# Laying the first half's mLSTM stage between the attention units of a one-core decoder layer

## Chip, cores and metric

One core of a Trainium2 chip runs the whole layer in one launch. The metric is device time in microseconds (us) from launch to the last result; lower is better. The engines are PE (TensorE, matmuls and transposes), DVE (VectorE), ACT (ScalarE), POOL (GpSimd) and SP (SyncE, which only issues DMAs). Each takes its own instructions strictly in order; they meet only at semaphores.

## What is computed

The reference is a decoder layer on x of 8 batches x 128 tokens x 128 features, with three residual blocks, each behind a layer norm without weights:

```python
x = x + attn(layernorm(x))            # 16 heads of 8, causal, "hyperbolic" distances:
#   d2 = |q|^2 - 2 q.k + |k|^2 ; ed = sqrt(d2) ; ns = |q|^2 + |k|^2
#   dist = where(ed<0.1, taylor, where(ed>2, 0.693+log(ed)+c*ns/4, ed*sqrt(1+c*ns)))
#   o = softmax(-beta*dist, causal) @ v ; then o @ Wo.T
x = x + mlstm(layernorm(x), ctx, ctx) # 4 heads of 32, q = norm(x), k = v = ctx
#   ig, fg = [q,k,v] @ kernel + bias ;  cs = cumsum(log_sigmoid(fg))        (per head, over tokens)
#   log_D[s,t] = cs[s] - cs[t] + ig[t] (t<=s) ;  m[s] = max_t log_D
#   C = (q.k/sqrt(32)) * exp(log_D - m) ;  n = max(|sum_t C|, exp(-m)) ;  h = C/(n+1e-6) @ v
#   then a layer norm of each head times a scale
x = x + moe(layernorm(x))             # 8 experts of 256, top 2, silu(g)*u, all experts computed
```

With a[t] = ig[t] - cs[t] the decay exponent becomes a[t] - runmax[s], where runmax is the running maximum of a, and m = cs + runmax. That form is used before and after.

## The kernel before

**Three stretches.** The attention is 16 units (`NU`); a unit is half the heads of one batch. Then come the mLSTM stage and the experts, both in two halves (`NCH` = 2 chunks `c` of 4 batches). A half of the mLSTM stage is `front(c, k)` (norm, transpose, gates, running sum and maximum), then per batch `rows(m)` and `outs(m)` (m = 0..3 for half 0, 4..7 for half 1), then `back(c, k)` (head norm, residual, next layer norm, transpose, router). The experts are passes z = 0..15: 8 experts over half 0, then 8 over half 1. `back(1, k)` is laid between passes z = 2 to 9.

**The attention is software-pipelined.** Each engine has a function `step(s)`, s = -1 (PE: -2) to 20, and in step s works on several units. In step s, in the order of each engine:

- DVE: copies PV's result of unit s-4 (`o_sb`, where it ends a batch), `da` of s (L927), `sel` of s (L932, a predicated copy), two reduces of the distance of s-2 into `nm` (L942, L944), `prod` of s (L949), `o_n` (L953), `x1` = x + attention (L965), `m_ge` of s+1 (L970), `dist` of s-1 (L981, a predicated copy).
- ACT: `e2` (L676) and `l1` (L681) of s+1, `pT` (exp, L686) of s-3, `oT` (L690), `sqn` of s+1 (L695), `lp` of s (L700), `wt` of s+1 (L704), `shift` of s-2 (L709), `ds` of s (L713).
- PE: scores n1 of s+1 (needs `sel` of s), scores d2 of s+2, the output product Wo, 24 PV matmuls of s-3, the transpose of `nm` of s-2 (into bank `PM`), the transposes of `dist` of s-2 with its shift (into `P3`), the transpose of `o_n`.
- POOL: adds the causal mask to `dist` of s-1 (L531, L532), then `m_gt` of s+1 (L540, one long compare).

Four steps stand in a hardware loop body: `steps` runs s = 5..12 as two iterations of four. After steps 13 to 19 `ACT_TAIL`, `DVE_TAIL` and `PE_TAIL` name the few parts of half 0 that follow: the norm after steps 13 and 14, the gates and the running sum after step 18 on DVE, `rows(0)` after step 19. `rows(1..3)`, `outs(0..3)`, `back(0, .)` and the whole of half 1 come after the steps, in an order written out by hand for each engine.

**The gates before.** PE forms them as 36 rows (heads in rows 0 to 3 and 32 to 35) by 512 tokens in one bank. DVE and ACT then work on 4 partitions x 512 elements: ACT abs, exp, ln (L734 to L737); DVE min, subtract, four scans for the running sum (L997 to L1002), `arow`, four scans for the running maximum (L1008 to L1011), a last add (L1013). PE transposes `arow` back to tokens, ACT copies it out (L740), and only then `rows` can start. ACT also spreads the transposed norm into a block-diagonal tile `xblk` (L727, four copies). In PE's `rows(m)`, per head a mask matmul and a matmul that subtracts the running maximum go into `exp_bank(m)`, then one wide product q.k goes into bank `P2`; ACT takes four exps (L749); DVE multiplies (L1020, `cT`); PE's `outs(m)` multiplies by ctx; DVE copies (L1026, `hs`).

**Other parts the change touches.** The values of v are copied from `vab` to `v_st` by DMA, two batches at a time, in SP's queue between the loads of the score stacks. POOL clears `arow`, `w1_mem` and `xblk[0]` behind its step 5 (L553 to L555), and clears `xblk[1]` and copies ctx (L565, L567) behind its last step. ACT's `l1`, `sqn` and `wt` take bias, or bias and scale, from columns of the constant tile `cf`:

```python
A(l1[:, p, :], e2[:, p, :], ACT.Ln, scale=LN_SHIFT, bias=col(K_SEPS))
A(row(sqn), ps2, ACT.Square, scale=col(K_R8), bias=col(K_R8))
A(wt[:, p, :], sqn[:, :], ACT.Square, bias=col(K_HALF))
```

Of the kernel before, what the change touches and what calls it, by code (L numbers as in the profile page):

```python
# [7 lines left out]
NT = B * S  # L8
# [23 lines left out]
ACT_TAIL = {13: [("front", 0, 0)], 15: [("front", 0, 2)], 16: [("front", 0, 3)], 19: [("front", 0, 4), ("rows", 0)]}  # L32
DVE_TAIL = {13: [("front", 0, 0)], 14: [("front", 0, 1)], 18: [("front", 0, 3)], 19: [("rows", 0)]}
PE_TAIL = {14: [("front", 0, 1)], 15: [("front", 0, 2)], 19: [("front", 0, 4), ("rows", 0)]}
# [12 lines left out]
C_COL = C_NSEL + XH  # L47
# [14 lines left out]
def constants():  # L62
# [8 lines left out]
    for h in range(XH):  # L71
        c[h, C_NSEL + h] = -1.0
# [25 lines left out]
    return c, b.astype(mybir.dt.np(mybir.dt.bfloat16))  # L98
# [16 lines left out]
def decoder_layer(nc, x, ctx, ctx_t, wq_t, wk_t, wv_t, wo_t, log_c, log_beta, ig_k, ig_b, fg_k, fg_b,  # L115
                  norm_scale, router_t, gate_w, gate_b, up_w, up_b, down_w, down_b,
                  const_f, const_b, stack_init, out):
# [5 lines left out]
    with es:  # L123
# [11 lines left out]
        def sem(name):  # L135
# [62 lines left out]
        v_st = [sb(f"v_st{k}", [128, PB, 144]) for k in range(2)]  # L198
# [10 lines left out]
        dist = sb("dist", [128, 4, UW])  # L209
# [11 lines left out]
        xblk = [over(split_mem, [128, CB, XH, S]), over(dist_mem, [128, CB, XH, S], at=4 * NT)]  # L221
        frow = over(split_mem, [36, 2, CT], at=3072)
        lf = over(proj_mem, [4, CT], at=4 * CT)
        cs = over(proj_mem, [4, CT], at=5 * CT)
        runmax_all = [over(w1_mem, [128, CT], at=c * CT) for c in range(NCH)]
        runmax = [t[0:4, :] for t in runmax_all]
        arow = over(proj_mem, [36, CT], at=7 * CT)
        aT = sb("aT", [128, NCH, CB, 36])
        enm = sb("enm", [128, NCH, CB, XH])
        dT = over(split_mem, [128, 2, XH, S], at=4096)  # L230
        cT = over(split_mem, [128, 2, XH, S], at=5120)
        hs = over(dist_mem, [128, CB, XH, XD + 1], at=6 * NT)
        hden = sb("hden", [128, 3, CB * XH])
# [3 lines left out]
        hst = over(dist_mem, [128, 8, CB * XH], at=6 * NT + 640)  # L237
# [25 lines left out]
        names = ("cf_in par_in cb_in wqkv_in misc_in ctx_in exp_in stack0 v0_in v1_in out_done qsplit_done "  # L263
# [4 lines left out]
                 "x1_done gt_done causal_done nmT_full t_full pv_done oT_full wo_full g_full abs_done l1p_done "  # L268
                 "a_done rT_full aT_done enm_done ex_full dT_done cT_done hs_done hq_done hr_done lg_full "
# [54 lines left out]
        def steps(eng, step, first, last, lo, hi, after):  # L324


            for s in range(first, lo):
                step(At(None, s))
            with eng.Fori(0, (hi - lo + 1) // 4) as i:
                for j in range(4):  # L330
                    step(At(i, lo + j))
            for s in range(hi + 1, NU + 5):
                if s <= last:
                    step(At(None, s))
                after(s)
# [51 lines left out]

        def exp_bank(m):

            return (P1 if m < CB else P3)[:, m % 2, :]  # L390

        def cross_bank(m):

            return (PO, PM)[m % 2][:, :] if m < CB else P1[:, m % 2, :]

        def back_banks(c):

            return (PM[:, :], PO[:, :]) if c == 0 else (P3[:, 0, :], P3[:, 1, :])
# [3 lines left out]
        def _(sp):  # L402
# [71 lines left out]
            sp.wait_ge(sm["v_done"], 2)  # L474
# [7 lines left out]
            for k in range(2):  # L482
                next_values(NP - 1, k)
# [11 lines left out]
        def _(pool):  # L495
            link = linker(pool, "chain_p")
            pool.memset(eps_col[:, :], LN_EPS)
            pool.memset(wg_raw[:, :, :], 0.0).then_inc(sm["init_done"], 1)
# [44 lines left out]
            def zeros(s):  # L543
                if s == 5:
# [951 lines left out]
```

## Time and profile before

| | before |
|---|---|
| time, median of 3 runs | 296.92 us (296.44 to 297.27) |
| the profiled execution: its own time | 297.92 us |
| its span, first to last instruction | 296.1 us |
| busy PE / DVE / ACT / POOL | 225.9 / 220.1 / 170.9 / 108.9 us |
| mean granted TensorE clock | 0.764 of full speed |
| first attention scores (PE) | 33.38 us |
| first expert matmul (PE) | 202.47 us |

Busy time is an average over stretches with different limits, so the stretches are read apart: attention from 33 us, its last steps and the mLSTM stage from about 120 to 202 us, the experts after that. The granted clock is given as a share of 2.4 GHz: 0.50 is 1.2 GHz, 1.00 is 2.4 GHz, and values between are a stretch that had some of both. Bracketed text at the end of a timeline row is how long that engine had stood idle and whose result ended it.

### The profile page before, as it was taken

What the parts mean: (1) busy time and instruction counts of PE and PEld (TensorE: products, weight loads), DVE (VectorE), ACT (ScalarE), POOL (GpSimd) and SP (SyncE); (2) the same over time, 40 slices, a digit from 0 to 9 for tenths busy, and PEclk for the clock granted to TensorE, in tenths of its full rate; (3) what the DMA queues carried; (4) which work ended last, traced back from release to release, by engine and by line L of the source; (5) the groups of instructions that cost most, each with busy time, mean ns of one, the idle gap of its engine ahead of it and who ended that gap; (6) DMA issues with size and microseconds to landing.
All of it is one profiled execution on the core that took longest, in us unless ns stands there. A gap on an engine that the chain in (4) does not pass through costs nothing.

```text
span 296.1 us, 5262 instructions
## 1 busy us (share of the span) xinstructions
PE 225.9 (76%) x1624; PEld 180.5 (61%) x1624; DVE 220.1 (74%) x544; ACT 170.9 (58%) x291; POOL 108.9 (37%) x140
## 2 busy tenths in 40 slices
PE   0768323889897878779658950997994999999994
PEld 0423222777686767564536720685893889888984
DVE  6777699998989989993591658387669967656554
ACT  3498899999899999937412561355131137232330
POOL 5233235777756766552830000001042224334400
PEclk9995555575557785555856995699599699999999
DMA  5309779770413300086000000000000000010001
GB/s 156 79 1 194 164 183 231 182 212 24 95 18 81 71 24 20 0 251 196 2 1 0 0 0 0 3 0 1 2 0 0 0 2 1 2 35 0 0 0 35
DMA packets 38084, 16.80 MB, mean 57 GB/s; under 512 B 19240, under 2 KB 36016, under 8 KB 38064
## 3 DMA queue, kind: packets, MB, share of 16 engines
q1 hardware_dynamic: 38064, 16.56, 22.4%
q8 instruction: 10, 0.16, 0.2%
q14 instruction: 10, 0.08, 0.1%
HBM read 10.39 MB, written 4.98 MB: 52 GB/s over the span
## 4 chain that ended last, share of the span: by engine, by line
PE 41%; DVE 19%; issue 13%; ACT 13%; POOL 8%; DMA 4%; SPq 1%; DVEq 0%; ACTq 0%; POOLq 0%
PE P L1180 29%; PE PM L1180 6%; PE PO L1180 6%; POOL m_gt L540 5%; ACT sqn L695 2%; POOL dist L532 2%; DVE dist_mem L932 2%; DMA stn<-n_split 1%; ACT dist_mem L676 1%; POOL dist L531 1%; DMA k_split<-split_mem 1%; DVE proj_mem L1002 1%; ACT dist_mem L704 1%; DMA x_sb<-x 1%; DVE dist L981 1%
## 5 line engine op out<-in xcount | busy, mean ns | idle before, releaser
L782 ACT ACTIVATE dist_mem<-P,gub 128x512 f32<-128x512 f32 x32 | 21.8, 687 | 54.5 <-PE P L1180 54.5
L579 POOL CAST whi<-wgu 128x512 fp32r (+1 forms) x16 | 10.3, 642 | 101.5 <-PE P L1180 101.5
L1109 DVE SCALAR_TENSOR_TENSOR dist_mem<-P,gub,dist_mem 128x512 f32<-128x512 f32 x32 | 23.6, 749 | 23.0 <-ACT dist_mem L782 23.0
L540 POOL TENSOR_SCALAR m_gt<-dist_mem 128x768 uint8<-128x768 f32 x16 | 34.3, 2145 | 8.2 <-issue 5.9
L1180 PE MATMUL P<-cf,dist 128*128 128x128 f32 x96 | 29.5, 392 | 8.9 <-ACT shift L709 8.9
L1180 PE MATMUL P<-xhi,whi 128*128 128x512 f32 x64 | 28.5, 446 | 4.6 <-DVE dist_mem L1109 4.0
L531 POOL TENSOR_TENSOR dist<-dist,cf 128x128 f32<-128x128 f32 x32 | 14.6, 457 | 41.2 <-DVE dist L981 41.2
L1180 PEld LDWEIGHTS P<-cf,dist 128*128 128x128 f32 x96 | 19.1, 199 | 15.5 <-ACT shift L709 11.5
L1180 PE MATMUL PO<-v_st,pT 128*64 128x9 f32 (+1 forms) x384 | 25.6, 241 | 3.4 <-ACT pT L686 3.4
L1180 PEld LDWEIGHTS PO<-v_st,pT 128*64 128x64 f32 x384 | 23.9, 187 | 6.3 <-ACT pT L686 3.9
L1180 PE MATMUL P<-xhi,wlo 128*128 128x512 f32 x64 | 26.9, 421 | 0.0
L1180 PE MATMUL P<-xlo,whi 128*128 128x512 f32 x64 | 26.9, 420 | 0.0
L1180 PE MATMUL P<-shift,cb 128*128 128x128 bf16 x96 | 26.8, 289 | 0.0
L1180 PE MATMUL P<-stn,stq 128*128 128x128 bf16 (+1 forms) x128 | 12.8, 271 | 12.9 <-DVE dist_mem L932 12.9
L582 POOL TENSOR_TENSOR wlo<-wgu,whi 128x512 fp32r<-128x512 f32 x16 | 20.7, 1293 | 2.9 <-POOL whi L579 2.9
L1180 PEld LDWEIGHTS P<-stn,stq 128*128 128x128 bf16 x128 | 10.5, 133 | 15.0 <-issue 14.6
L1180 PEld LDWEIGHTS P<-xhi,whi 128*128 128x128 f32 x64 | 13.1, 205 | 7.7 <-issue 5.3
L932 DVE COPY_PREDICATED dist_mem<-m_ge,P 128x768 f32<-128x768 uint8 x16 | 16.3, 1017 | 1.2 <-ACT dist_mem L704 1.2
L927 DVE SCALAR_TENSOR_TENSOR dist_mem<-dist_mem,P 128x768 f32<-128x768 f32 x16 | 15.2, 950 | 2.2 <-ACT sqn L695 1.4
L1180 PEld LDWEIGHTS PO<-proj_mem,dist_mem 128*128 128x128 f32 x128 | 16.0, 196 | 0.7
L1180 PEld LDWEIGHTS PM<-proj_mem,dist_mem 128*128 128x128 f32 x128 | 15.9, 196 | 0.9 <-DVE dist_mem L1109 0.3
L686 ACT ACTIVATE pT<-P,nbeta 128x768 f32<-128x768 f32 x16 | 14.2, 887 | 3.9 <-PE P L1180 3.8
(219 smaller groups left out, 592.2 us busy)
## 6 DMA issues: line engine op xcount, KB each, us to landing
q_split<-split_mem SPq DMA_DIRECT2D x16, 128.0 KB, 2.7
k_split<-split_mem SPq DMA_DIRECT2D x4, 512.0 KB, 3.6
stq<-q_split SPq DMA_DIRECT2D x16, 128.0 KB
stk<-k_split SPq DMA_DIRECT2D x16, 128.0 KB
v_st<-vab SPq DMA_DIRECT2D x8, 144.0 KB, 2.3
wgu<-gate_w SPq DMA_DIRECT2D x1, 1024.0 KB, 5.8
wgu<-up_w SPq DMA_DIRECT2D x1, 1024.0 KB, 9.4
x_sb<-x SPq DMA_DIRECT2D x2, 256.0 KB, 3.1
```

The lines of the kernel that those rows point to most:

```text
L531: pool.tensor_tensor(wideq, wideq, cm, ALU.add)
L532: last = pool.tensor_tensor(near, near, cm, ALU.add)
L540: pool.tensor_scalar(m_gt[:, g.k % 2, :], e2[:, g.k % 2, :], 4.0 - ATT_EPS, None, ALU.is_gt).then_inc(sm["gt_done"], 1)
L579: pool.tensor_copy(hi, w).then_inc(sm["whi_done"], 1)
L582: pool.tensor_tensor(lo, w, hi, ALU.subtract).then_inc(sm["w_ready"], 1)
L686: A(row(pT, t.k % 2), P3[:, :, 0:384], ACT.Exp, scale=nbeta[:, :]).then_inc(sm["pT_done"], 1)
L695: A(row(sqn), ps2, ACT.Square, scale=col(K_R8), bias=col(K_R8)).then_inc(sm["sqn_done"], 1)
L782: A(sil[:, f, :], P[:, 0, :], ACT.Silu, bias=gub[:, 0, bass.ds(e * FC + f, 1)]).then_inc(sm["sil_done"], 1)
L927: V.scalar_tensor_tensor(row(da, p), row(l1, p), 2.0, n1, ALU.mult, ALU.add).then_inc(sm["da_done"], 1)
L932: V.copy_predicated(row(wt, p), row(m_ge, p), n1).then_inc(sm["sel_done"], 1)
L1109: V.scalar_tensor_tensor(hT[:, 2 * slot + f, :], (P1, P2)[f][:, 1, :], gub[:, 1, bass.ds(e * FC + f, 1)], sil[:, f, :], ALU.add, ALU.mult) ...
L1180: return nc.tensor.matmul(out_, lhsT, rhs, start=start, stop=stop, **more)
```

## The change

- The loops over attention steps are written out (`steps` is a plain Python loop), and each engine's step has numbered places 1 to 7; tables `ACT_AT`, `DVE_AT`, `PE_AT` name what is laid at `(step, place)`.
- Half 0's mLSTM stage goes there: the statistics of each batch (`stat(b)`) in steps 8 to 12, the norm in step 13, the gates in step 14, running maximum and the first exponents in step 15, `rows`/`outs` 0 to 3 in steps 15 to 19, the head norm's start in 19 and 20. Half 1's statistics are in step 20.
- The gates are formed as tokens (partitions) by 8 numbers per batch: eight matmuls of 8 columns in place of two pairs of 512 columns. The running sum is one product with a triangular matrix `tri` over 16 columns. One transpose to 16 rows, one scan of 16 x 128 for the running maximum, one transpose back.
- `rows` on PE is split into `ex(m)` and `qk(m)`; q.k has one bank for each half (`P2` bank 0, `PM`), `outs` another.
- POOL writes the block-diagonal tile from SBUF (`blocks(c)`), half 0 behind its step 14, and copies ctx behind its step 10. The clearing of `arow` and `w1_mem` is gone.
- PV reads `vab` itself; the DMAs to `v_st` are gone. `l1`, `sqn`, `wt` take constants as numbers.
- The head norm subtracts the mean before it divides by the normalizer, and folds the normalizer in later.

```diff
+ACT_AT = {(13, 1): [("front", 0, 0)], (13, 7): [("front", 0, 2)], (14, 4): [("front", 0, 3)],
+          (15, 5): [("rows", 0)], (16, 2): [("front", 0, 4), ("rows", 1)], (16, 7): [("rows", 2)], (17, 7): [("rows", 3)],
+          (20, 7): [("front", 1, 0)]}
+DVE_AT = {(8, 7): [("stat", 0)], (9, 7): [("stat", 1)], (11, 7): [("stat", 2)], (12, 6): [("stat", 3)],
+          (13, 3): [("front", 0, 1)], (14, 3): [("front", 0, 3)], (14, 6): [("front", 0, 4)], (15, 1): [("front", 0, 5)],
+          (15, 5): [("front", 0, 6)], (15, 7): [("stat", 4)], (16, 5): [("rows", 0)], (16, 7): [("stat", 5), ("rows", 1), ("outs", 0)],
+          (17, 7): [("rows", 2), ("outs", 1)], (18, 7): [("rows", 3), ("outs", 2)], (19, 7): [("outs", 3), ("back", 0, 0)],
+          (20, 7): [("stat", 6), ("stat", 7), ("back", 0, 1)]}
+PE_AT = {(13, 5): [("front", 0, 1)], (14, 1): [("front", 0, 2)], (14, 4): [("front", 0, 3)], (14, 5): [("front", 0, 4)],
+         (15, 3): [("front", 0, 5), ("ex", 0)], (15, 5): [("ex", 1), ("qk", 0)], (16, 5): [("ex", 2), ("outs", 0), ("qk", 1)],
+         (17, 5): [("ex", 3), ("outs", 1), ("qk", 2)], (18, 5): [("outs", 2), ("qk", 3)], (19, 5): [("outs", 3)]}
...
-            with sp.Fori(2, NP) as bp:
+            for bp in range(2, NP):
                 for k in range(2):
                     next_stack(bp, k)
-                    next_values(bp - 1, k)
...
-                    pool.memset(arow[:, :], 0.0)
-                    pool.memset(w1_mem[:, :], 0.0)
                     pool.memset(xblk[0][:, :, :, :], 0.0).then_inc(sm["xblk0"], 1)
+            def blocks(c):
+                pool.wait_ge(sm["xT_done"], NO[1, c] + 1)
+                for h in range(XH):
+                    r = slice(h * XD, (h + 1) * XD)
+                    link(pool.tensor_copy(xblk[c][r, :, h, :], tok(xT, c)[r, :].rearrange("p (b s) -> p b s", b=CB)))
+                pool.sem_inc(sm["blk_done"], 1)
...
-                    A(l1[:, p, :], e2[:, p, :], ACT.Ln, scale=LN_SHIFT, bias=col(K_SEPS)).then_inc(sm["l1_done"], 1)
+                    A(l1[:, p, :], e2[:, p, :], ACT.Ln, scale=LN_SHIFT, bias=LN_SHIFT * ATT_EPS).then_inc(sm["l1_done"], 1)
-                    A(row(sqn), ps2, ACT.Square, scale=col(K_R8), bias=col(K_R8)).then_inc(sm["sqn_done"], 1)
+                    A(row(sqn), ps2, ACT.Square, scale=8 ** -0.5, bias=8 ** -0.5).then_inc(sm["sqn_done"], 1)
...
+            # DVE, front(c, k)
                 if k == 3:
+                    dve.wait_ge(sm["g_full"], c + 1)
+                    V.tensor_tensor(gpre[:, c, :, :], G[:, 0:32]..., gb[:, :]..., ALU.add).then_inc(sm["pre_done"], 1)
+                    link(V.tensor_scalar(f[1], gpre[:, c, :, XH:], 0.0, None, ALU.min))
+                if k == 4:
+                    dve.wait_ge(sm["l1p_done"], c + 1)
+                    V.tensor_tensor(gf[:, c, 2, :], gf[:, c, 1, :], gf[:, c, 0, :], ALU.subtract).then_inc(sm["lf_done"], 1)
+                    dve.wait_ge(sm["cs_full"], c + 1)
+                    V.tensor_copy(gf[:, c, 1, :], G[:, 32:48])
+                    V.tensor_tensor(aT[:, c, :]..., gpre[:, c, :, 0:XH], G[:, 32:48]..., ALU.subtract).then_inc(sm["aT_done"], 1)
+                if k == 5:
+                    dve.wait_ge(sm["ar_full"], c + 1)
+                    V.tensor_tensor_scan(runmax[:, c, :], R, one, -3e38, ALU.max, ALU.mult).then_inc(sm["rm_done"], 1)
...
+            # PE, front(c, k)
                 if k == 2:
-                    mm(G[0:36, :], wg[:, 0, :], tok(xT, c), stop=False)
-                    mm(G[0:36, :], wg[:, 1, :], tok(ctxT, c), start=False).then_inc(sm["g_full"], 1)
+                    for b in range(CB):
+                        mm(G[:, cols], tok(xT, c, b), wg_raw[:, 0, :], stop=False)
+                        last = mm(G[:, cols], tok(ctxT, c, b), wg[:, :], start=False)
+                if k == 3:
+                    mm(G[:, 32:48], tri[:, :], gf[:, c, 2, :]).then_inc(sm["cs_full"], 1)
+            def ex(m):   # waits rm_done (b = 0), em_done (b = 1), dT_done of m-2 (b >= 2)
+            def qk(m):   # waits blk_done and sel_done >= NU (m = 0), x1_done (m = 4), cT_done >= m
+                mm(qk_bank(m), tok(ctxT, c, b), xblk[c][:, b].rearrange("p h s -> p (h s)"))
```

The hand-written order behind the steps, now for half 1 with `back(0, .)` between:

```diff
-            steps(pe, step, -2, NU + 4, 5, 12, after)
-            rows(1) rows(2) outs(0) rows(3) outs(1) front(1, 1) outs(2) front(1, 2) outs(3) front(1, 4)
-            rows(4) rows(5) rows(6) outs(4) outs(5) rows(7) back(0, 5) outs(6) back(0, 6) outs(7)
+            steps(step, -2, NU + 4)
+            front(1, 1) front(1, 2) front(1, 3) front(1, 4) front(1, 5)
+            ex(4) qk(4) ex(5) back(0, 5) outs(4) qk(5) ex(6) back(0, 6) outs(5) qk(6) ex(7) outs(6) qk(7) outs(7)
```

## Rows read from the trace of the kernel before

**Rows 1.** Stretches: length, busy of PE, PEld, DVE, ACT, POOL; clock, DMA share, GB/s.

```profile
77.00:113.30 36.30, 30.47 (x330) 25.69 (x328) 33.98 (x67) 35.19 (x53) 22.99 (x31) 0.69 0.21 50
...
141.80:162.00 20.20, 13.45 (x102) 10.16 (x102) 11.19 (x25) 6.33 (x15) 8.75 (x10) 0.66 0.00 1
162.00:185.50 23.50, 12.68 (x84) 9.32 (x82) 15.43 (x46) 10.25 (x26) 0.00 (x0) 0.83 0.00 0
```

**Rows 2.** ACT's instructions grouped by line and shape: busy us, mean ns.

```profile
L695 ACT ACTIVATE sqn<-P,cf 128x768 f32<-128x768 f32 x16 | 15.7, 984 | 0.5 <-PE P L1180 0.5
L681 ACT ACTIVATE dist_mem<-dist_mem,cf 128x768 f32<-128x768 f32 x16 | 15.0, 936 | 0.5
...
L700 ACT ACTIVATE lp<-dist_mem 128x768 f32<-128x768 f32 x16 | 13.4, 838 | 3.5 <-DVE dist_mem L949 3.5
```

**Rows 3.** Timeline of DVE, attention steps 8, 13, 15: start us, us, what.

```profile
83.55 0.95 DVE L927 SCALAR_TENSOR_TENSOR dist_mem<-dist_mem,P 128x768 f32<-128x768 f32 x1
...
113.34 0.95 DVE L927 SCALAR_TENSOR_TENSOR dist_mem<-dist_mem,P 128x768 f32<-128x768 f32 x1
...
129.20 0.94 DVE L927 SCALAR_TENSOR_TENSOR dist_mem<-dist_mem,P 128x768 f32<-128x768 f32 x1
...
140.73 1.02 DVE L981 COPY_PREDICATED dist<-m_gt,dist_mem 128x768 f32<-128x768 uint8 x1
```

**Rows 4.** Timeline of DVE beside POOL's work, steps 6 and 13.

```profile
73.41 2.53 DVE L970 TENSOR_SCALAR m_ge<-dist_mem 128x768 uint8<-128x768 f32 x1
...
116.04 0.94 DVE L949 SCALAR_TENSOR_TENSOR dist_mem<-dist_mem 128x768 f32<-128x768 f32 x1
```

**Rows 5.** Timeline of POOL at the same two places.

```profile
73.72 1.80 POOL L555 MEMSET split_mem<- 128x2048 f32 x1
...
115.08 2.13 POOL L540 TENSOR_SCALAR m_gt<-dist_mem 128x768 uint8<-128x768 f32 x1
```

**Rows 6.** Timeline of DVE: norms, gate work, head norm, outside the attention's own instructions.

```profile
127.04 2.02 DVE L873 TENSOR_SCALAR xn<-x_sb,mv,rs 128x128 f32<-128x128 f32 x4
...
147.16 0.74 DVE L997 TENSOR_SCALAR split_mem<-P,gb 4x512 f32<-4x512 f32 x1
...
153.72 0.68 DVE L1013 TENSOR_TENSOR proj_mem<-proj_mem,w_mem 4x512 f32<-4x512 f32 x1
...
164.96 0.86 DVE L860 BATCH_NORM_STATS2 bst<-x_sb 128x6 f32<-128x128 f32 x4
...
167.69 1.11 DVE L873 TENSOR_SCALAR xn<-x_sb,mv,rs 128x128 f32<-128x128 f32 x4
...
174.11 0.30 DVE L1026 COPY dist_mem<-PM 128x132 f32<-128x132 f32 x1 [1.96 <-PE PM L1180]
...
177.03 0.69 DVE L1046 TENSOR_TENSOR split_mem<-split_mem,dist_mem 128x512 f32<-128x512 f32 x1
```

**Rows 7.** Timeline of PE: gates, PV, half 1's first rows, last outs, first expert.

```profile
136.50 1.92 PE L1180 MATMUL P<-xT,wg 128*36 128x512 f32 x2
...
145.04 1.13 PE L1180 MATMUL PO<-v_st,pT 128*64 128x9 f32 x24 [1.80 <-ACT pT L686]
...
184.55 0.61 PE L1180 MATMUL P<-cf,proj_mem 36*128 36x36 f32 x4 [10.48 <-DVE proj_mem L1013]
185.55 0.29 PE L1180 MATMUL P<-cb 128*128 128x128 bf16 x1 [0.38 <-ACT aT L740]
...
196.43 0.22 PE L1180 MATMUL P<-cb 128*128 128x128 bf16 x1
...
197.76 1.02 PE L1180 MATMUL P<-dist_mem,split_mem 128*128 128x512 f32 x2
...
199.91 1.06 PE L1180 MATMUL PO<-rw,dist_mem 128*128 128x8 f32 x8
200.82 1.06 PE L1180 MATMUL P<-ctx,split_mem 128*128 128x33 f32 x8
202.47 0.47 PE L1180 MATMUL P<-xhi,whi 128*128 128x512 f32 x1 [0.59 <-DVE dist_mem L1026]
```

More of the change, by code:

```diff
@@ L70, in constants @@
     c[:, C_CM:C_CM + HALF] = np.where(np.arange(HALF)[None, :] > (p % HALF)[:, None], FAR, 0.0)
-    for h in range(XH):
+    for h in range(CB * XH):
         c[h, C_NSEL + h] = -1.0
@@ L322, in pass_waits, with steps @@
             eng.sem_inc(sm["passed"], 1)
-        def steps(eng, step, first, last, lo, hi, after):
-            for s in range(first, lo):
+        def steps(step, first, last):
+            for s in range(first, last + 1):
                 step(At(None, s))
[L329 to L335, printed above, removed]
         def linker(eng, name):
@@ L585, in _ @@
             prepare(1, 1, 1)
+            pool.wait_ge(sm["t_full"], NU)
+            link(pool.memset(xblk[1][:, :, :, :], 0.0))
+            blocks(1)
             with pool.Fori(1, E // 2) as i:
@@ L662, in _, with at @@
                 last.then_inc(sm["v_done"], 1)
+            def at(s, place):
+                stages = dict(front=front, rows=rows, back=back)
+                for stage, *which in ACT_AT.get((s, place), ()):
+                    stages[stage](*which)
             def step(s):
+                k_ = s.k
                 u, t = s + 1, s - 3
@@ L783, in silu @@
                       bias=gub[:, 0, bass.ds(e * FC + f, 1)]).then_inc(sm["sil_done"], 1)
-            def after(s):
-                stages = dict(front=front, rows=rows, back=back)
-                for stage, *which in ACT_TAIL.get(s, ()):
-                    stages[stage](*which)
-            steps(act, step, -1, NU + 4, 5, 12, after)
-            rows(1)
-            front(1, 0)
-            rows(2)
-            rows(3)
+            steps(step, -1, NU + 4)
+            back(0, 0)
             front(1, 2)
+            back(0, 1)
             front(1, 3)
-            front(1, 5)
-            back(0, 0)
-            back(0, 1)
+            back(0, 2)
             front(1, 4)
@@ L905, in _, with at @@
                 V.tensor_scalar(nsl[:, c, :], ksl[:, :], col(K_M36), None, ALU.mult).then_inc(sm["split_done"], 1)
+            def at(s, place):
+                stages = dict(front=front, rows=rows, outs=outs, back=back, stat=stat)
+                for stage, *which in DVE_AT.get((s, place), ()):
+                    stages[stage](*which)
             def step(s):
+                k_ = s.k
                 def row(t, w):
@@ L1125, in weigh @@
                 last.then_inc(sm["y_done"], 1)
-            def after(s):
-                stages = dict(front=front, rows=rows, outs=outs, back=back)
-                for stage, *which in DVE_TAIL.get(s, ()):
-                    stages[stage](*which)
-            steps(dve, step, -1, NU + 4, 5, 12, after)
-            rows(1)
-            front(1, 0)
-            front(1, 1)
-            outs(0)
-            rows(2)
-            outs(1)
-            outs(2)
-            rows(3)
-            outs(3)
-            back(0, 0)
+            steps(step, -1, NU + 4)
+            front(1, 1)
+            back(0, 2)
             front(1, 3)
-            back(0, 1)
+            back(0, 3)
+            front(1, 4)
             front(1, 5)
+            front(1, 6)
+            back(0, 5)
             rows(4)
-            back(0, 2)
+            outs(4)
             rows(5)
-            back(0, 3)
-            outs(4)
-            back(0, 5)
+            outs(5)
+            back(0, 6)
             rows(6)
-            outs(5)
+            outs(6)
             rows(7)
-            outs(6)
-            back(0, 6)
             outs(7)
@@ L1226, in pair_count, with at @@
                 return m if u.i is None else u.i * each + m
+            def at(s, place):
+                stages = dict(front=front, ex=ex, qk=qk, outs=outs, back=back)
+                for stage, *which in PE_AT.get((s, place), ()):
+                    stages[stage](*which)
             def step(s):
+                k_ = s.k
                 u = s + 1
@@ L1423, in down @@
                 last.then_inc(sm["y_full"], 1)
[L1425 to L1435 removed]
+            steps(step, -2, NU + 4)
             front(1, 1)
[L1437 removed]
             front(1, 2)
[L1439 removed]
+            front(1, 3)
             front(1, 4)
[L1441 to L1443 removed]
+            front(1, 5)
+            ex(4)
+            qk(4)
+            ex(5)
+            back(0, 5)
             outs(4)
+            qk(5)
+            ex(6)
+            back(0, 6)
             outs(5)
[L1446 to L1447 removed]
+            qk(6)
+            ex(7)
             outs(6)
[L1449 removed]
+            qk(7)
             outs(7)
```

330 lines of the change are left out of this document (162 added, 168 removed).

## The prediction

> **What bounds the kernel now.** I read the stretches first [rows 1]. In attention steps 7 to 12 (77 to 113.3 us) ACT is busy 35.19 of 36.30 us, DVE 33.98, PE 30.47 at a mean clock of 0.69: ACT leads, DVE is 2.3 us behind it, and nobody has room. From 141.8 us to 185.5 us it is the reverse: 43.7 us in which DVE works 26.6, PE 26.1 and ACT 16.6. This stretch is a chain of waits, and that is where the change works. The DMA share there is 0.00, so the expert weights have long landed; loading them earlier, or sparing the `v_st` loads, buys nothing by itself. What makes the chain long is read in the timelines. DVE spends 147.16 to 154.40 us on half 0's gate rows, tiles of 4 partitions by 512, before it takes up the attention's last units [rows 6]. Later PE stands idle 10.48 us until DVE's L1013 has finished the same work for half 1, and starts its rows at 185.55 [rows 7]. Half 0's `rows` and `outs` run only after the attention steps, ending with DVE's copy at 174.11 [rows 6]. PE begins the experts at 202.47 [rows 7]. Behind that point nothing in the change alters the work of a pass.
>
> I count as three intervals. T is the end of the last `dist` copy on DVE (before: 140.73 + 1.02 = 141.75 [rows 3]); S is PE's first exponent matmul for batch 4 (185.55); M is the first expert matmul (202.47) [rows 7]. So before T to S is 43.8 us and S to M is 16.9 us.
>
> **1. Up to step 13 (`da` at 113.34 before [rows 3]).** Constants given as numbers: `l1` takes 936 ns and `lp`, the same work without a column operand, 838 [rows 2], so one such operand costs 0.10 us. `wt` loses one as well, `sqn` loses two (984 against 838 is 0.15, two operands would be 0.20). That is 0.35 to 0.40 us per unit on ACT. In steps 0 to 5, where DVE's load is lighter since `nm` and `o` are not there at first, I take 1.5 us of the possible 2.3 (bounds 0 and 2.3). In steps 7 to 12 DVE becomes the bound after 2.3 us [rows 1], and it is given four `stat(b)`: four statistics took 0.86 us together [rows 6], single ones each with a wait and an aggregate I take at 0.5, so 2.0 us (bounds 0.9 and 2.4). Six steps cost DVE 36.0 against 36.3 before: -0.2 (bounds -1.4 and +1.5).
>
> The cleared tiles: `m_ge` took 2.53 us from 73.41 [rows 4] and ended 0.4 us behind POOL's memset of `xblk` (73.72 to 75.52 [rows 5]). That memset, 2048 elements in 1.80 us, stays; the two that go (512 and 1024 elements) are 1.35 us at that rate. I take -1.0 (bounds 0 and -1.35), because PE has nearly as much to do there. Unrolling by itself, the 8-column gate weights formed at the start and the fewer DMAs: 0. The time between `da` of step 8 and of step 13, 83.55 to 113.34, is 5.96 us a step [rows 3], all of it accounted for by busy ACT and DVE, so a loop branch costs nothing to be won. The page "Runtime: NRT & Kernel Launch" of the Trainium skill (Instruction fetch mechanics) says that a taken branch out of the fetched window stalls the fetch and that kernels prefer unrolling for it; by that rule there would be a gain here, and the trace does not show one to be had. `da(13)`: 113.34 - 1.5 - 1.0 - 0.2 = 110.6.
>
> **2. Steps 13 and 14.** Before they took 15.9 us (113.34 to 129.20 [rows 3]), with half 0's statistics and norm in them. The norm stays (its four `xn` 2.02 us [rows 6]), the statistics leave (-1.2). New: in step 14 DVE waits at place 3 for the gates. PE forms them in 8 matmuls of 8 columns, each two instructions. The router's 8 instructions of that form, begun at 199.91, gave way to the next at 200.82 [rows 7]: 0.11 each at full clock, so 16 are 1.8 us, and 3.6 at half clock. The wide form cost 2 x 1.92 at most [rows 7], so on PE it is a draw; but now PV of unit 11, the `nm` transpose and DVE's `prod`, `m_ge` and `dist` stand behind it. I take +3.0 us (bounds 1.2 and 3.6). Then DVE waits in place 6 for three small ACT functions and for the triangular product and holds up `dist`: +1.2 (bounds 0.4 and 2.0). Six small DVE operations of 8 to 32 columns: the 132-column copy takes 0.30 [rows 6], I take 0.2 each, +1.2 (bounds 0.6 and 1.8). 15.9 - 1.2 + 3.0 + 1.2 + 1.2 = 20.1, `da(15)` at 130.7.
>
> **3. `da(15)` to T.** Before 12.55 us [rows 3], with the wide gates inside, 136.50 to about 139.9, ahead of Wo and PV on PE [rows 7]: -3.4. New on PE ahead of the last `dist`: `ex(0)`, `ex(1)`, `qk(0)`. An `ex` is 196.43 to 197.76, so 1.33 us; a `qk` 1.02 [rows 7], 0.9 start to start: +3.6, and DVE's `cT(0)`, +0.7. T = 130.7 + 13.4 = 144.1 (bounds: none of it visible 140; PE at half clock 148). POOL's four block copies stand behind `m_gt`, ahead of the next causal mask. They are hidden unless they end late; bound 0 to 2.4.
>
> These copies and the ctx copy also run beside DVE. A long POOL compare, 115.08 to 117.21 [rows 5], left DVE's two-input `prod` at 0.94 us, begun inside it at 116.04 [rows 4], while the memset did hold up `m_ge`. The Trainium skill's "SBUF — State Buffer" (two separate sides) says the port that DVE and GpSimd share is locked for a whole instruction, also against a DVE operation with two SBUF inputs when GpSimd reads SBUF. By that rule the copies would add up to their own 3.4 us; by the row, only one-input operations suffer. My sum has 0 for it and the bound above.
>
> **4. T to S.** PE has still: `ex` 2, 3 (2.7), `outs` 0 to 3 (1.06 [rows 7], 0.9 start to start: 3.6), `qk` 1 to 3 (2.7), PV of three units (1.13 each [rows 7]: 3.4), two units' transposes, which I estimate as long as PV with its hand-over (2.6), and some 1.5 for hand-overs: 16.5 us at full clock, in place of the same work one after the other behind the steps. Then a DVE chain: head norm start as from 174.41 to 177.72 before [rows 6], less one multiply of 0.7 (2.6); the last `x1` and half 1's statistics to `xn`, as 164.96 to 168.80 [rows 6] (4.1); the square on ACT and two reductions between them (1.9). PE has idled, so half clock: transposes and copy 1.2, gates 3.6; then sign, exp, ln 1.5; triangular product, copies, transpose, scan 2.0. 16.5 + 8.6 + 8.3 = 33.4 against 43.8 (bounds 29 and 38, by 0.1 or 0.3 us per small operation and the clock). The 7.24 us block and its twin are gone from the chain; `back(0,2)` and `back(0,3)` fill DVE's waits. S = 177.5.
>
> **5. S to M and on.** The same matmuls, with q.k in one bank, `qk(m)` waiting for `cT(m-1)`: 0.9 + 0.7 plus hand-overs is under the 3.1 us of PE a batch, hidden. 16.9 stays (bounds 14.5 and 18.5): M = 194.4, 8.1 us earlier. The experts' 93.6 us stay.
>
> **Sum.** The profiled execution took 297.92 (span 296.1), 1.0 above the median of 296.92. The same 8.1 us off gives 289.8 and 288.8; I say 288.8.
>
> **Rivals.**
> - *PE stays at half clock through the laid stage* (slower than before). The attention ran at a mean of 0.69, the next stretch at 0.66 [rows 1]. The 16.5 us of part 4 would be 33, since ex, outs and qk stand in PE's queue ahead of `nm` and PV, the attention's own chain: +14 to 16, 303 us. It decides above 8.1 us, that is if half of this work runs at half clock. Against: as PE gets denser (162 to 185.5, where rows and outs follow each other) the clock was 0.83 [rows 1]. Chance 0.10.
> - *Order waits eat half*: DVE, strictly in order, waits at place 3, 6 and 7 for PE and ACT, each time with the attention's `dist` or `nm` behind it, 4 us more than counted: 292.8. For it: part 3 and 4 leave each hand-over 0.1 to 0.2 us. Chance 0.20.
> - *Nothing to be seen*: what half 0 gains is given back because PE waits in S for half 1's norm anyway and the early part is lengthened by 8 us of stall: 296.9. Chance 0.04.
> - *More*: PE at full clock for both gates (-3.6), constants pay in all steps (-2): 283. Chance 0.14.
> - *Forecast*, 285.5 to 291: chance 0.52.
>
> **How the numbers follow.** A measurement of this kernel tells about 0.3% (0.9 us) from nothing. Faster: forecast, more, order waits, 0.86 in all; same 0.04; slower 0.10. The range reaches from the lower case's 283 to the end of the order waits at 295: 282.8 to 295.0, which leaves 0.14 above and some 0.05 below.
>
> **What the profile after would show.** `sqn` near 0.79 us, `l1` and `wt` near 0.84; `m_ge` of step 6 under 1.6; `da(13)` near 110.6; an idle of DVE of 1 to 3.5 us in step 14 ended by PE; no DVE operation on 4 x 512; T near 144; S near 177.5, M near 194.4. Wrong if PE's clock in 135 to 160 us is near 0.5, if T comes after 150, or if the expert passes take longer than 93.6 us.

## The result, and the profile after

The changed kernel takes 330.52 us (median of 4 runs, 329.93 to 333.15) against 297.10 for the kernel before (4 runs, 296.44 to 297.49): ratio 1.1168, 95% interval 1.1126 to 1.1210, so 33.4 us slower. The prediction had 288.8 us in 282.8 to 295.0, with 0.10 for slower. Times are medians of all runs of a kernel, ratios leave out runs over 1.5% above that kernel's fastest; this matters for two kernels below, whose medians without such runs are 296.1 us (f7_grouped128) and 282.4 (g1_best). The profiled execution took 330.08 us, its span 328.2.

The same stretches as in [rows 1], and one more, from half 1's first exponent product to the first expert matmul (columns as there):

```profile
core 0 of [0], span 328.2 us
core 0: us, PE busy (x) PEld busy (x) DVE busy (x) ACT busy (x) POOL busy (x), PEclk, DMA share, GB/s
77.00:113.30 36.30, 28.08 (x338) 23.24 (x337) 35.64 (x77) 34.60 (x54) 24.54 (x32) 0.78 0.44 119
141.80:162.00 20.20, 19.35 (x98) 12.91 (x97) 4.14 (x11) 3.79 (x13) 5.32 (x8) 0.50 0.00 1
162.00:185.50 23.50, 19.08 (x83) 13.36 (x83) 6.60 (x23) 2.75 (x8) 1.80 (x1) 0.50 0.00 0
201.00:234.70 33.70, 32.28 (x102) 21.16 (x101) 6.66 (x22) 5.91 (x19) 0.00 (x0) 0.50 0.00 0
```

In steps 7 to 12 all is as planned: DVE is now the fuller engine. From 141.8 us on the picture turns. PE, 13.45 us busy in the second stretch before, is busy 19.35 of 20.20, and its clock is at 0.50, the 1.2 GHz level. In the last stretch PE is busy 32.28 of 33.70 us and the clock does not rise either; the kernel before did that work in 16.9 us, with PE no less busy for its length but at a clock of 0.84:

```profile
185.50:202.50 17.00, 16.36 (x101) 13.14 (x101) 10.32 (x35) 6.40 (x21) 0.00 (x0) 0.84 0.00 1
```

The three marks of the prediction, in DVE's and PE's timelines (start us, us, engine line, operation):

```profile
109.33 0.95 DVE L925 SCALAR_TENSOR_TENSOR dist_mem<-dist_mem,P 128x768 f32<-128x768 f32 x1
...
123.72 0.19 DVE L1004 TENSOR_TENSOR gpre<-P,gb 128x32 f32<-128x32 f32 x1 [3.71 <-PE P L1176]
...
128.88 0.95 DVE L925 SCALAR_TENSOR_TENSOR dist_mem<-dist_mem,P 128x768 f32<-128x768 f32 x1
...
148.98 1.01 DVE L986 COPY_PREDICATED dist<-m_gt,dist_mem 128x768 f32<-128x768 uint8 x1
...
185.19 0.29 DVE L968 TENSOR_TENSOR x_sb<-PM,x_sb 128x128 f32<-128x128 f32 x1
```

```profile
200.99 0.29 PE L1176 MATMUL P<-cb 128*128 128x128 bf16 x1
201.21 0.79 PE L1176 MATMUL P<-runmax,cf 16*128 16x128 f32 x2
201.93 0.29 PE L1176 MATMUL P<-cb 128*128 128x128 bf16 x1
...
234.69 0.76 PE L1176 MATMUL P<-xhi,whi 128*128 128x512 f32 x1 [0.64 <-issue]
```

So `da(13)` at 109.3 and `da(15)` at 128.9 come 1.3 and 1.8 us before the forecast, T is 150.0 (144.1), S 201.0 (177.5) and M 234.7 (194.4). All of the loss arises behind 129 us. And the second fence shows what the text of the change hardly says: the pick product of an exponent bank, `pick` times `runmax`, now sums over 16 rows. Before, the same product was this:

```profile
158.36 0.31 PE L1180 MATMUL P<-cb 128*128 128x128 bf16 x1
158.47 0.74 PE L1180 MATMUL P<-w_mem,cf 128*128 128x128 f32 x2
159.00 0.31 PE L1180 MATMUL P<-cb 128*128 128x128 bf16 x1
```

Over 128 rows mask and pick of one head take 159.00 - 158.36 = 0.64 us at the half clock; over 16 rows 201.93 - 200.99 = 0.94 (0.64 + 0.30). All 64 picks lie where the clock is 0.50 (mean of one instruction 497 ns; before 354, some of them at the full clock). One `ex` is four of these: 3.76 us, where the prediction had 1.33.

### The profile page after: what moved, and what is told of

Its sections match the earlier page's. It is cut to its first block, busy times and chain, and to the rows that moved or that the text cites. A ratio compares the mean times of both kernels' runs of the same rounds, so it can differ in the third digit from the quotient of the medians.

```text
span 328.2 us, 5128 instructions
## 1 busy us (share of the span) xinstructions
PE 254.6 (78%) x1648; PEld 198.0 (60%) x1648; DVE 210.0 (64%) x535; ACT 157.9 (48%) x281; POOL 112.8 (34%) x145
## 4 chain that ended last, share of the span: by engine, by line
PE 55%; DVE 21%; issue 8%; POOL 6%; ACT 5%; DMA 3%; SPq 1%; DVEq 0%; ACTq 0%; POOLq 0%
PE P L1176 39%; PE PM L1176 9%; PE PO L1176 8%; POOL m_gt L531 3%; DVE dist L986 3%; DVE dist_mem L932 2%; POOL dist L522 1%; POOL dist L523 1%; DVE xn L863 1%; DMA stn<-n_split 1%; DMA k_split<-split_mem 1%; DVE dist_mem L951 1%; DMA x_sb<-x 1%; DVE nm L943 1%; DVE dist_mem L1118 1%
## 5 line engine op out<-in xcount | busy, mean ns | idle before, releaser
L1176 PE MATMUL P<-xhi,whi 128*128 128x512 f32 x64 | 28.1, 440 | 5.1 <-DVE dist_mem L1118 4.4
L749 ACT ACTIVATE split_mem<-P,aT 128x128 f32<-128x128 f32 x32 | 9.1, 368 | 36.9 <-PE P L1176 36.9
L1176 PEld LDWEIGHTS PO<-vab,pT 128*64 128x64 f32 x384 | 22.1, 175 | 7.2 <-issue 5.0
L1176 PE MATMUL PO<-vab,pT 128*64 128x9 f32 (+1 forms) x384 | 23.8, 233 | 2.1 <-DVE o_sb L918 1.3
L1176 PE MATMUL P<-runmax,cf 16*128 16x128 f32 x64 | 25.3, 497 | 0.0
L1176 PEld LDWEIGHTS P<-runmax,cf 16*128 16x128 f32 x64 | 15.9, 306 | 6.4 <-issue 3.4
L1176 PEld LDWEIGHTS P<-stn,stq 128*128 128x128 bf16 x128 | 9.8, 129 | 15.4 <-issue 15.1
L1029 DVE SCALAR_TENSOR_TENSOR split_mem<-P,split_mem 128x512 f32<-128x512 f32 x4 | 2.8, 688 | 25.1 <-PE P L1176 25.1
L705 ACT ACTIVATE lp<-dist_mem 128x768 f32<-128x768 f32 x16 | 13.5, 842 | 6.4 <-DVE dist_mem L951 6.3
```

The costliest lines, as they stand in the source:

```text
L705: A(lp[:, :], prod[:, s.k % 2, :], ACT.Ln, scale=16.0).then_inc(sm["lp_done"], 1)
L749: last = A(dT[:, m % 2, h, :], exp_bank(m)[:, h * S:(h + 1) * S], ACT.Exp, bias=aT[:, m // CB, at_:at_ + 1])
L1176: return nc.tensor.matmul(out_, lhsT, rhs, start=start, stop=stop, **more)
```

## The experiments

In the table, S is PE's first product for batch 4 and M its first expert matmul, as in the prediction; S to M was 16.9 us before and 33.7 in the changed kernel. Each ratio is against the kernel before, measured anew beside it.

| kernel | us | ratio (95%) | S | M |
|---|---|---|---|---|
| before | 297.1 | 1 | 185.6 | 202.5 |
| changed | 330.5 | 1.117 (1.113, 1.121) | 201.0 | 234.7 |
| e1_rows128 | 301.1 | 1.015 (1.009, 1.021) | 190.0 | 207.0 |
| e8_rows96 | 303.5 | one run | 191.3 | 210.0 |
| e2_rows64 | 333.5 | one run | 203.7 | 237.4 |
| e3_before16 | 329.0 | 1.104 (1.099, 1.109) | 203.6 | 236.1 |
| e4_behind | 340.9 | one run | 211.3 | 245.0 |
| e5_behind128 | 309.5 | 1.043 (1.039, 1.047) | 200.0 | 216.9 |
| f6_grouped16 | 321.0 | one run | 196.8 | 225.6 |
| g2_grouped64 | 320.6 | one run | 195.5 | 224.3 |
| f7_grouped128 | 298.3 | 0.998 (0.995, 1.002) | 186.8 | 202.9 |
| g3_half1of16 | 320.3 | one run | 190.3 | 224.0 |
| f9_later | 293.0 | 0.989 (0.986, 0.993) | 170.3 | 196.2 |
| g1_best | 283.5 | 0.950 (0.947, 0.953) | 172.9 | 192.5 |

**Theory A: the rows.** Products that sum over few rows hold the granted clock at 0.50, and cost more each besides. **Theory B: the laying.** Work between the units, with its order and its gaps, keeps the clock low. The first four kernels part them.

**e1_rows128 and e2_rows64.** `K` is 128 or 64:

```
-        runmax = sb("runmax", [CB * XH, NCH, S])
+        runmax = sb("runmax", [K, NCH, S])
...
+            pool.memset(runmax[:, :, :], 0.0)
...
-                    V.tensor_tensor_scan(runmax[:, c, :], R, ...
+                    V.tensor_tensor_scan(runmax[0:CB * XH, c, :], R, ...
...
-                    pick = cf[0:CB * XH, one:one + 1].to_broadcast([CB * XH, S])
+                    pick = cf[0:K, one:one + 1].to_broadcast([K, S])
```

> The changed kernel, but the product that spreads the running maximum (the ex matmuls) has all 128 rows again as its length of sum: the 16 rows of runmax are padded with zeros to 128, and the one-hot column is read over 128 rows. The values are the same; GpSimd clears the tile once, before the steps. Theory A (short operands: the 64 ex matmuls of 16 rows keep TensorE's granted clock at 0.50 from 130 us on, and are slower each): the granted clock rises to above 0.8 in most of the laid stage's part after 140 us, the pick matmul falls from 497 to about 350 ns, from the first ex of half 1 to the first expert matmul it takes 17 to 20 us in place of 33.7, and the kernel takes 295 to 306 us. Theory B (laying the stage between the units keeps the clock low, whatever the operands): clock stays at 0.50, 33 us stay 31 to 34, kernel 325 to 331 us.

> The same with 64 rows in place of 128. Theory A in its graded form (the more rows work, the sooner the clock rises): between the changed kernel's 330.5 us and the one with 128 rows, near the latter, 297 to 315 us. If the rows count only by a whole step (full or not), 325 us or more. Theory B: 325 to 331 us.

With 128 rows 301.14 us: 29.4 of the 33.4 us are gone, by zeros. The stretches of e1_rows128:

```profile
core 0 of [0], span 298.7 us
core 0: us, PE busy (x) PEld busy (x) DVE busy (x) ACT busy (x) POOL busy (x), PEclk, DMA share, GB/s
...
141.80:162.00 20.20, 17.42 (x130) 12.91 (x128) 4.87 (x13) 5.82 (x18) 7.16 (x9) 0.75 0.00 1
162.00:185.50 23.50, 13.91 (x68) 11.31 (x68) 12.86 (x43) 2.59 (x8) 2.51 (x4) 0.50 0.00 1
190.00:207.00 17.00, 15.55 (x102) 12.50 (x101) 6.76 (x23) 5.91 (x19) 0.00 (x0) 0.90 0.00 0
```

The last stretch is back at 17.0 us and a clock of 0.90. With 64 rows nothing is won (333.5; the pick 498 ns on average against 497): the graded form of theory A is wrong.

**e3_before16.** The kernel before, and one thing changed:

```
-                    pick = cf[:, C_NSEL + h:C_NSEL + h + 1].to_broadcast([128, S])
-                    last = mm(..., pick, runmax_all[c][:, b * S:(b + 1) * S], start=False)
+                    pick = cf[0:16, C_NSEL + h:C_NSEL + h + 1].to_broadcast([16, S])
+                    last = mm(..., pick, runmax_all[c][0:16, b * S:(b + 1) * S], start=False)
```

> The kernel before with one edit: the 64 pick matmuls sum over the first 16 rows in place of 128 (the other 112 rows of the one-hot column are zero, so the values are the same). Nothing is laid, nothing moved. Theory A: the clock that rises to full near 156 us stays at 0.50 until the experts, the 16.9 us from the first ex of half 1 to the first expert matmul become 26 to 32, half 0 loses 5 to 10 as well, and the kernel takes 310 to 325 us. Theory B: 296 to 299 us.

328.96 us against 297.36 beside it: these two lines alone cost 31.6 us, somewhat more than I expected of them. Its stretches from each half's first `ex` on:

```profile
core 0 of [0], span 328.1 us
core 0: us, PE busy (x) PEld busy (x) DVE busy (x) ACT busy (x) POOL busy (x), PEclk, DMA share, GB/s
...
158.00:185.50 27.50, 27.50 (x82) 17.34 (x82) 5.70 (x22) 5.68 (x21) 0.00 (x0) 0.50 0.00 0
203.80:236.00 32.20, 31.68 (x100) 21.29 (x99) 10.03 (x34) 6.31 (x21) 0.00 (x0) 0.50 0.00 0
```

PE is busy in 27.50 of 27.50 us, the clock is 0.50, and nothing is laid here. Theory B falls as the cause of this loss; what the laying does by itself is read at 128 rows.

**e4_behind and e5_behind128.** The tables of the changed kernel flattened: every piece of half 0's stage stands behind the last step, in unchanged order; e5_behind128 has the 128 rows as well.

```
-ACT_AT = {(13, 1): [("front", 0, 0)], (13, 7): [("front", 0, 2)], ...
+ACT_AT = {(20, 7): [("front", 0, 0), ("front", 0, 2), ("front", 0, 3), ("rows", 0), ...
-                if s == 14:
-                    blocks(0)
+            blocks(0)
             prepare(0, 0, 0)
```

> The changed kernel with all pieces of the first half's xLSTM stage in the same order but behind the last step of the units, none between them (PE, DVE and ACT; GpSimd's blocks too). All other parts of the change stay: token-major gates, triangular product, 16-row ex, new banks, unrolled steps, constants of ScalarE. Theory A: the steps end near 147 us or sooner, the clock stays at 0.50 through both halves' ex products, and the kernel takes 315 to 330 us. Theory B: without the laying the clock is that of before, and the kernel takes 292 to 302 us.

> The first half's stage behind the last step, as in the earlier run of that kind, but with the ex products over 128 rows. It prices the laying alone, with the clock no longer held down. If laying gains (what the prediction took), this is slower than the laid form with 128 rows (301.1 us): 304 to 312 us. If the laid pieces cost as much in the steps as they save behind them, 299 to 304 us. If the laying itself is a loss, under 298 us. The last copy of distances should end near 131 us as in the earlier run (laid with 128 rows: 146.3).

340.9 us with 16 rows, above both ranges, and 309.5 with 128. The rows cost 31.4 us here too, so 29.4, 31.6 and 31.4 in three kernels of different order. S to M says it most plainly: 16.9 to 17.0 us with 128 rows in all three, 32.5 to 33.8 with 16 or 64. And at 128 rows laying gains 8.4 us over not laying (301.1 against 309.5), though it does not beat the kernel before, in which part of half 0's stage (norm, gates, scans [rows 6]) stood within the steps already.

**e8_rows96.** The same edit with `K` = 96.

> The changed kernel with runmax padded to 96 rows. With 64 rows it took 333.5 us, as with 16; with 128 rows 301.1. If any product of less than all 128 rows is of the other kind (A1): 326 to 334 us, pick near 497 ns. If the rows count by their number from some point on: 300 to 320 us.

303.5 us, and the clock from S to M is 0.82; each mask and pick of the first `ex` behind S take 0.62 to 0.64 us, as over 128 rows. Between 64 and 96 rows lies a step; neither the number of rows nor "less than all" is what counts. This is where the Trainium skill helps: "TensorEngine Tiling (Array Packing)" (When to Use Tiling) has a row-tiled form for a sum over 64 rows and another for 32, and (Key Properties) says that changing the tiling mode drains TensorE. Nothing in the kernel asks for a tile, but the step at 64 to 96 is where that page has it. The loads of weights show something like the drain (first the changed kernel, then e1_rows128):

```profile
201.93 0.11 PEld L1176 LDWEIGHTS P<-cb 128*128 128x128 bf16 x1 [0.22 <-issue]
202.15 0.50 PEld L1176 LDWEIGHTS P<-runmax,cf 16*128 16x128 f32 x2
202.87 0.11 PEld L1176 LDWEIGHTS P<-cb 128*128 128x128 bf16 x1 [0.22 <-issue]
```

```profile
155.93 0.55 PEld L1177 LDWEIGHTS P<-runmax,cf 128*128 128x128 f32 x2
156.36 0.15 PEld L1177 LDWEIGHTS P<-cb 128*128 128x128 bf16 x1
156.57 0.55 PEld L1177 LDWEIGHTS P<-runmax,cf 128*128 128x128 f32 x2
```

With 128 rows the load for the mask begins at 156.36, while the pick is still running (the mask's matmul starts at 156.57). With 16 rows it begins at 201.93, together with its own matmul, after 0.22 us of idle: nothing is loaded ahead across a change of kind (from a sum over up to 64 rows to one over 128, or back). That could explain the price of each, and perhaps also the clock. So the next pair changes kinds less often.

**f6_grouped16 and f7_grouped128.** One mask matmul for the four heads:

```
-                for h in range(XH):
-                    mm(exp_bank(m)[:, h * S:(h + 1) * S], ident_b, cb[:, B_MASK:B_MASK + S], stop=False)
+                mask = cb[:, B_MASK:B_MASK + S].rearrange("p (o s) -> p o s", o=1).to_broadcast([128, XH, S])
+                mm(exp_bank(m)[:, 0:XH * S].rearrange("p (h s) -> p h s", h=XH), ident_b, mask, stop=False)
+                for h in range(XH):
...
-                    last = mm(..., pick, runmax[:, c, :], start=False)
+                    last = mm(..., pick, runmax[:, c, :], start=False, stop=(h == XH - 1))
```

> The changed kernel with 16-row picks, but one mask matmul over all four heads (512 columns) ahead of the four picks, so that a 128-row product and a 16-row one follow each other once in an ex in place of four times. 96 rows gave 303 us, 64 gave 333, so rows up to 64 are of another kind than rows from 96 on. Theory A1 (it is the switch between the two kinds that costs, because the weight load of the other kind isn't begun under the matmul before it): one ex falls from 3.76 us at half clock (4 x 0.94) to about 2.6 us, the clock rises at least in parts after 140 us, and the kernel takes 300 to 318 us. Theory A2 (it is the few rows of the pick themselves): the clock stays at 0.50, the pick keeps its 497 ns at half clock, and the kernel takes 322 to 330 us.

> The laid form with 128 rows, and the one mask matmul over the four heads. Against 301.1 us: one ex is 4 x 0.53 + 0.43 = 2.55 us at half clock, as before (2.56), so that nothing is won in PE's time; 299 to 303 us under both theories. It is the control for the same edit with 16 rows.

f6_grouped16 took 320.99 us. One of its `ex`, one of f7_grouped128 at the same clock of 0.50, and the stretches of f6_grouped16:

```profile
208.10 0.63 PE L1176 MATMUL P<-cb 128*128 128x512 bf16 x1
208.66 2.07 PE L1176 MATMUL P<-runmax,cf 16*128 16x128 f32 x8
210.66 0.59 PE L1176 MATMUL P<-rw,dist_mem 128*128 128x8 f32 x2
```

```profile
142.85 0.63 PE L1177 MATMUL P<-cb 128*128 128x512 bf16 x1
143.28 1.91 PE L1177 MATMUL P<-runmax,cf 128*128 128x128 f32 x8
144.99 1.34 PE L1177 MATMUL P<-split_mem 128*128 128x512 f32 x2
```

```profile
core 0 of [0], span 319.1 us
core 0: us, PE busy (x) PEld busy (x) DVE busy (x) ACT busy (x) POOL busy (x), PEclk, DMA share, GB/s
141.00:160.00 19.00, 17.47 (x95) 12.32 (x96) 4.39 (x12) 4.30 (x14) 5.33 (x8) 0.50 0.00 1
160.00:185.00 25.00, 17.56 (x79) 12.71 (x79) 8.64 (x31) 3.50 (x10) 1.80 (x1) 0.50 0.00 0
197.30:225.60 28.30, 26.91 (x88) 18.92 (x87) 6.28 (x19) 5.73 (x19) 0.00 (x0) 0.50 0.00 1
```

With one change of kind in place of four, the `ex` fell from 3.76 to 210.66 - 208.10 = 2.56 us. The same form over 128 rows takes 144.99 - 142.85 = 2.14. The eight picks themselves are nearly as long (2.07 against 1.91 us); most of the 0.42 us lies before the first pick and behind the last, so it is mainly the change of kind that costs, and not the product. ("TensorE: Matmul & The Clock Gate", Why this matters for your kernels, of the Trainium skill says that a single matmul over 32 rows takes the time of one over 128; the eight picks agree with that nearly.)

But the clock stayed at 0.50. So there are two effects, and A1 was right about the smaller alone. The one mask is worth 330.5 - 321.0 = 9.5 us with 16 rows and 301.1 - 298.3 = 2.8 us with 128, where no change of kind is spared; the difference of 6.7 us is what the spared changes are worth. The rows cost another 321.0 - 298.3 = 22.7 us between two kernels that differ in the rows of the pick alone. At most some 3.4 of these (eight `ex`, 0.42 us each) are the change of kind that is left; the rest goes with the clock. f7_grouped128 scattered from 294.3 to 302.7 us in ten runs and f6_grouped16 is one run, so these differences are good to a few us only.

f7_grouped128 was meant as a control without effect, and that was a wrong sum: I expected 2.55 us for its `ex` at the half clock, as for four masks and four picks (4 x 0.64 = 2.56), and it takes 2.14. Eight times 0.42 us is 3.4 at the half clock and less at the full one, about what it gained.

**g2_grouped64 and g3_half1of16.** The grouped form with `K` = 64; and e1_rows128 with 16 rows in half 1 alone:

```
+                    K = 128 if c == 0 else 16
+                    pick = cf[0:K, one:one + 1].to_broadcast([K, S])
+                    last = mm(..., pick, runmax[0:K, c, :], start=False)
```

> One mask matmul per ex and 64-row picks. With 16 rows this form took 320.99 us, the ex at half clock 2.56 us as with 128 rows, and yet the clock stayed at 0.50 up to 215 us; with 128 rows it took 298.3. If the rows that work count by their number (theory C), 64 is between the two: 300 to 316 us with the clock above 0.50 in parts after 140 us. If products of up to 64 rows are simply the other kind: 319 to 323 us.

> The laid form with 128 rows in half 0's ex products and 16 in half 1's. If what the short operands do is bound to where they stand: up to the first ex of half 1 as with 128 rows (190 us), from there to the first expert matmul 30 to 34 us as in the changed kernel (33.5) in place of 16.9, kernel 315 to 319 us. If the loss of half 1 came from the state in which half 0's stage left the clock: 300 to 305 us.

64 rows: 320.6 us, as with 16, and S to M is 28.8 us in both. But its clock did rise once, while half 0's last `ex` ran and behind it, which that of the 16-row form did not:

```profile
160.00:185.00 25.00, 15.45 (x105) 11.30 (x104) 11.96 (x41) 3.77 (x11) 1.80 (x1) 0.64 0.00 0
```

So 64 rows hold the clock down nearly as 16 do, and the graded form of theory A is refuted by the times, not by every stretch. Half 1 alone: S at 190.3, as with 128 rows (190.0), then 33.7 us to M in place of 16.9: the loss of half 1 arises within half 1, it is not inherited. The kernel's 320.3 is 1.3 above the range; S and M are as expected of a loss that is bound to where the short products stand.

**f9_later and g1_best.** What is left at 128 rows is the order. In the kernel before the last `x1` (DVE's sum with the product with Wo) is done at 162.1, 20.3 us after T. In e1_rows128:

```profile
145.32 1.01 DVE L987 COPY_PREDICATED dist<-m_gt,dist_mem 128x768 f32<-128x768 uint8 x1
...
174.17 0.29 DVE L969 TENSOR_TENSOR x_sb<-PM,x_sb 128x128 f32<-128x128 f32 x1
```

28.1 us after T, since `ex`, `outs` and `qk` stand in PE's queue ahead of PV and Wo of the last units; then PE idles 6.76 us for `xn`. f9_later puts them into that hole:

```
-         (15, 3): [("front", 0, 5), ("ex", 0)], (15, 5): [("ex", 1), ("qk", 0)], (16, 5): [("ex", 2), ("outs", 0), ("qk", 1)],
-         (17, 5): [("ex", 3), ("outs", 1), ("qk", 2)], (18, 5): [("outs", 2), ("qk", 3)], (19, 5): [("outs", 3)]}
+         (15, 3): [("front", 0, 5)], (16, 5): [("ex", 0)], (17, 5): [("ex", 1), ("qk", 0)], (18, 5): [("outs", 0), ("qk", 1)],
+         (19, 5): [("ex", 2)], (20, 6): [("outs", 1), ("qk", 2), ("ex", 3), ("outs", 2), ("qk", 3)]}
...
             front(1, 2)
+            outs(3)
             front(1, 3)
```

with DVE's and ACT's tables to match, and the head norm of half 0 behind half 1's gates. g1_best adds the one mask matmul, and has half 0's `back` pieces on DVE straight behind `rows(4)`.

> 128 rows, and the pieces laid otherwise: half 0's gates and scan stay in steps 13 to 15, but its ex products start one step later, the third and fourth and two of the outs go behind the attention's last product with Wo, where PE stood idle 6.8 us (172.8 to 179.5), the last outs between the gates of half 1 and their triangular product (idle 3.0), and the head norm of half 0 moves on DVE and ACT from before half 1's gates to beside half 1's own ex products. In the laid form with 128 rows the last x1 was ready 27.9 us after the last copy of distances, in the kernel before 20.3. If it is the laid PE work at half clock ahead of the attention's last products that ate the gain: the last copy near 142, the last x1 near 163, first ex of half 1 near 181, first expert matmul near 199, kernel 290 to 296 us. If the work is only moved (PE at half clock still the bound), 299 to 303 us.

> The later-laid form (292.98 us) with the one mask matmul over the four heads, and in half 1's stretch the head norm, residual and row statistics of half 0 straight behind the first cT of half 1 on DVE, with the transposes before the last ex on PE. In the later-laid form PE stood idle 3.64 us for xn at 186.88, and the first expert matmul came 25.8 us after the first ex of half 1 (before: 16.9). If that norm held the experts back: 19 to 22 us, kernel 286 to 290 us. If PE's clock in that stretch decides (0.56 from 185 to 200 us): 291 to 295 us.

f9_later: the last `x1` at 158.4 (16.5 us after T), S 170.3, M 196.2, 292.98 us: faster than before by 1.1% (0.7 to 1.4). S came 11 us earlier than expected, but the head norm behind S then held up the transposes on PE; S to M was 25.9 us. g1_best brings that to 19.6 us: 283.51 us, ratio 0.950, better than both kernels and than I expected. Its profiled execution took 287.87 us, 4.4 above its median, so its S and M stand late. How its further 9.5 us divide between the mask and the order was not tried.

## Why the prediction was wrong

**Part 1 held, in part by luck.** `sqn` 804 ns and `l1` 844, as said, `da(13)` 109.3 against 110.6. Steps 8 to 13 took 29.8 us, as before (forecast 0.2 less). The other 4.0 us were gained up to `da(8)`, where I had 2.5: 1.1 of them stood at the first `da` already (the first scores came at 32.6 in place of 33.4, which is in no term), and 2.0 arose in steps 0 to 6 for 1.5. The cleared tiles were priced too high: `m_ge` of step 6 took 2.18 us, not under 1.6, since the memset of `xblk` still lies over it.

**Part 2 held.** 128.88 - 109.33 = 19.6 us for 20.1; the stall for the gates 3.71 for 3.0, just past the upper bound of 3.6.

**Part 3 failed first.** T came after 21.1 us, not 13.4. Two `ex` and a `qk` were set at 3.6 us from rows at the full clock with 128 rows; they were 2 x 3.76 + 1.9 = 9.4 us. With 128 rows (e1_rows128) it was 16.9 us, within my bound for PE at the half clock (148 - 130.7 = 17.3).

**Part 4 failed twice.** T to S was 51.0 us for 33.4. The term is "16.5 us at full clock": the clock was 0.50 throughout, and T to the last `x1` took 35.5 us. With 128 rows T to S was 43.7 us, still ten over, and T to the last `x1` 28.1: the clock was at 0.50 from 162 us on then as well, and the laid pieces stand in PE's queue ahead of the last PV and Wo. The DVE chain behind the last `x1` did shrink as said (before 185.55 - 162.07 = 23.5, in e1_rows128 190.0 - 174.5 = 15.5); the 8 us were given back ahead of it.

**Part 5 holds the step that decides.** "The same matmuls" was not so: the change cuts the sum of the pick product from 128 rows to 16, visible in the diff, and I priced it by the old form. "16.9 stays" became 33.7. The experts kept their time (93.5 for 93.6).

**The rival "PE stays at half clock"** had the right sign, the right place for part of the loss and a chance of 0.10; of the signs that I named for being wrong, the clock near 0.5 in 135 to 160 us came true. At 303 us it is close to what was measured with 128 rows, 301.1, but partly by luck: there the clock was 0.75 in 141.8 to 162 us, and part of the excess is the order, as f9_later shows. The kernel as it is lost the other 29.4 us by the rows, which neither forecast nor rival had. The argument against it, that a denser PE gets the clock, was read from 128-row products only.

What stays open is why up to 64 rows hold the clock down and 96 do not. Shown is that it is not PE's idle time (27.50 of 27.50 us busy in e3_before16), not the length of the products (2.07 against 1.91 us for eight), and not the order of the stage. Fewer changes of kind did not bring the clock back either, but no kernel had short products without any change, so a part of the changes in it is not excluded.

## What to carry to other kernels

In a diff, look at the number of rows that each matmul sums over, not only at its count and columns: an edit that makes an operand smaller can take the clock from everything around it, and padding with zeros to 128 rows gave back 29 of 33 us, to 96 rows 27. When work is laid between units, ask what stands behind it in the same queue: put it where the engine was seen idle, not ahead of the chain that ends last. And try the neutral form of the operand before the order: only with the clock restored could the order be judged; order and the one mask together then took 301.1 us to 283.5, 5% under the kernel before.

## What the hardware did that I had not expected

- Sums over 16 or 64 rows kept TensorE's granted clock at 0.50: over 16 rows through 27.50 us of unbroken PE work (e3_before16) whose other products had 128 rows, over 64 rows nearly throughout (g2_grouped64 had 0.64 in one stretch); with 128 rows the same stage reached 0.90. The page "TensorE: Matmul & The Clock Gate" (Part 1) of the Trainium skill has PE's own work release the clock and does not speak of rows; by it these stretches should have run at full, and the runs decide against that for such operands.
- A change between a sum over up to 64 rows and one over 128 cost 0.30 us per mask and pick at the half clock (0.94 against 0.64), and no weights were loaded ahead across it; with one such change in an `ex` in place of four, the `ex` was 0.42 us longer than over 128 rows (2.56 against 2.14) in place of 1.20.
